# End pass of a graph layer and expert layer: the second choice's scaling goes to GpSimd, and the last addition of a batch comes one batch later

## The chip, the cores and the metric

One core of one Trainium2 chip runs the whole kernel. The time is the device time of one execution in microseconds (us); lower is better. All arithmetic is in fp32.

## The reference, cut to what matters

Two layers run over 6250 nodes with 256 features each. The first gathers sums, maxima and means of the edges of each node and puts them through a two-layer network. The second is a mixture of experts with 16 experts, of which each node uses two. Only the end of the second layer is touched by the change:

```python
# x is the first layer's output plus its input ("x1" in the kernel)
n = _layernorm(x)                                    # "x2" in the kernel
topk_vals, topk_idx = jax.lax.top_k(n @ gate_w + gate_b, 2)
topk_w = jax.nn.softmax(topk_vals, axis=-1)
moe = jnp.sum(topk_w[..., None] * sel, axis=2)       # sel: rows of the two chosen experts
y = n + moe
mu, var = jnp.mean(y, -1, keepdims=True), jnp.var(y, -1, keepdims=True)
out = x + (y - mu) / jnp.sqrt(var + 1e-5) * gamma + beta
```

## The kernel before, in words

The nodes are cut into 50 tiles of 125 nodes, two tiles to a pair of 250 nodes, 25 pairs. The kernel runs in four stages: scans over the edges, the first layer pair by pair, the experts over 113 slot tiles of 128 rows (their outputs are scattered to a DRAM tensor `expert_rows`, first choices in one half and second choices in the other), and the end pass, which is the last 110 us or so. Only the end pass is changed.

The end pass runs over 14 batches (`BATCHES`, L145), numbered 0 to 13. Batches 0, 9 and 13 have one pair (two tiles), the other eleven have two pairs (four tiles). The values x1 of all nodes lie already in SBUF (`FX1`). The order of the work on each engine is written out by hand, and counting semaphores tie the engines together. For a batch n:

- **SyncE** (`load_y`, L494 to L512) loads the two expert rows of each node into `FY[n % 4][0]` and `FY[n % 4][1]`. Both loads add to the same semaphore `fy_got`. Four batches are loaded ahead. In the loop it waits for `f_read` n + 1 and loads batch n + 4, then waits for `f_out` n + 1 and stores batch n, with two transfers.
- **ScalarE** (L950 to L979) writes the normed rows into PSUM (`normed_again`, `FS[n % 2]`, signals `f_x2`), takes the square root of the variances (`deviation`, `f_sd`), and norms the finished sum from `FS` into `FN[n % 2]` in SBUF (`last_norm`, `f_norm`). Its order is normed_again 0, normed_again 1, deviation 0, last_norm 0, normed_again 2, deviation 1, last_norm 1, normed_again 3, and so on.
- **VectorE** (L1552 to L1601) adds the weighted expert rows onto `FS` in place (`add_expert(n, 0)` and `add_expert(n, 1)`, one SCALAR_TENSOR_TENSOR of 256 columns for each tile, L1559), takes mean and variance (`moments`, L1568 and L1571, `f_var`), works out scale and shift (`scale_shift`, L1578 and L1580, `f_stat`), and adds `FN` and the residual rows `FZ` into `FO` (`finish`, L1589, `f_out`).
- **GpSimd** (`times_gamma`, L698 to L705) multiplies `FN[n % 2]` by gamma in place, after `f_norm`, and signals `f_scaled`. It does nothing else in the end pass.
- **TensorE** (`residual_rows`, L1194 to L1206) writes x1 + beta into PSUM, `FZ[n % 2]`: for each pair a product with the identity over 512 columns (L1199) and two products of one row of ones with beta over 256 columns (L1201). From batch 2 on it waits for `f_out` n - 1, that is for `finish(n - 2)`, as there are two buffers. It signals `f_z`, for which `finish(n)` waits.

The loop of VectorE is, for n from 0 to 13: `add_expert(n + 1, 0)`, `scale_shift(n)`, `add_expert(n + 1, 1)`, `moments(n + 1)`, `finish(n)`.

Of the kernel before, what the change touches and what calls it, by code (L numbers as in the profile page):

```python
# [21 lines left out]
ALU = mybir.AluOpType  # L22
# [80 lines left out]
def gnn_moe_kernel(nc, x, dst, edge_attr, u, gW1, gb1, gW2, gb2, gate_w, gate_b,  # L103
# [3 lines left out]
    GF = u.shape[1]  # L107
    HID = gW1.shape[1]
    NX, _, FF = ew1.shape
    NT = 125  # L110
    TILES = N // NT
# [33 lines left out]
    BATCHES = [(0, 1)] + [(n, n + 2) for n in range(1, EARLY_M - 1, 2)] + [(EARLY_M - 1, EARLY_M)] + [(n, min(n + 2, MACROS)) for n in range(EARLY_M, MACROS, 2)]  # L145
# [4 lines left out]
    DEEP = 4  # L150
# [24 lines left out]
    def block_at(n):  # L175
        return n + LATE_M if n < EARLY_M else n - EARLY_M
# [10 lines left out]
    with ExitStack() as ctx:  # L187
        def sem(name):
            return ctx.enter_context(nc.semaphore(name))
# [30 lines left out]
        wsel = k.take(2, TILES, parts=NT)  # L220
# [8 lines left out]
        slotf, second = (k.take(SLOT_TILES) for _ in range(2))  # L229
# [11 lines left out]
        a = Area(mem, KEPT, A1)  # L241
# [4 lines left out]
        a = Area(mem, A1, TOTAL)  # L246
# [32 lines left out]
        a = Area(mem, WORK + 12 * D, WORK_END)  # L279
# [12 lines left out]
        a = Area(mem, WORK_END, TOTAL)  # L292
        OL = [a.take(OB, P, parts=NT) for _ in range(HOT)]
        OH = [a.take(OB, KINDS, parts=NT) for _ in range(HOT)]
        a = Area(mem, WORK_END, TOTAL)
        w1now = [a.take(DC, FF) for _ in range(4)]

        a = Area(mem, KEPT, W2_AT)
# [15 lines left out]
        a = Area(mem, at, W2_AT)  # L314
# [8 lines left out]
        a = Area(mem, W_AT, WORK)  # L323
# [6 lines left out]
        a = Area(mem, WORK, WORK_END)  # L330
        FX1 = [a.take(2 * (m1 - m0), D) for m0, m1 in BATCHES]

        a = Area(mem, W2_AT, A1)
        FY = [[a.take(CB, D) for _ in range(2)] for _ in range(DEEP)]
# [9 lines left out]
        FS, FZ = ([ps[0:NT, (at + 2 * b) * 512:(at + 2 * b + 2) * 512].rearrange("p (a d) -> p a d", a=CB) for b in range(2)] for at in (0, 4))  # L344
# [39 lines left out]
        yo_stored = [sem(f"expert_rows_stored{i}") for i in range(2)]  # L384
        fx_got = sem("final_x1_got")
        fy_got = [sem(f"final_y_got{i}") for i in range(DEEP)]
        f_x2, f_step, f_read, f_var, f_sd, f_stat, f_norm, f_scaled, f_z, f_out = (sem(f"final_{n}") for n in ("x2", "step", "y_read", "var", "sd", "stat", "norm", "scaled", "residual", "out"))
        pads_zeroed = sem("pads_zeroed")
        out_stored = [sem(f"out_stored{i}") for i in range(2)]
        passed = sem("waits_passed")  # L390
# [10 lines left out]
        def spread(ap, axis, n):  # L401

            shape = list(ap.shape)
            shape.insert(axis, n)
            return ap.unsqueeze(axis).to_broadcast(shape)
# [112 lines left out]
        def _(pool):  # L518
# [176 lines left out]
            in_pairs(pool, SLOT_TILES, slots_step, ahead=5, first=SURE - 4)  # L695


            def times_gamma(n):  # L698
                a = 2 * (BATCHES[n][1] - BATCHES[n][0])
                pool.wait_ge(f_norm, n + 1)  # L700
                pool.tensor_tensor(FN[n % 2][:, 0:a], FN[n % 2][:, 0:a], spread(gammabc, 1, a), ALU.mult).then_inc(f_scaled, 1)
            pool.wait_ge(yo_stored[0], (SLOT_TILES - SLOT_TILES // 2) * 16)
            pool.wait_ge(yo_stored[1], SLOT_TILES // 2 * 16)
            for n in range(len(BATCHES)):
                times_gamma(n)  # L705


        @block.scalar
        def _(act):
# [240 lines left out]
            def normed_again(n):  # L950
                m0, m1 = BATCHES[n]
                if n >= 2:
                    act.wait_ge(f_norm, n - 1)
                for a in range(2 * (m1 - m0)):
                    j = 2 * block_at(m0) + a
                    ins = act.activation(FS[n % 2][:, a, :], FX1[n][0:NT, a, :], ACT.Identity, bias=nmr_2[:, j:j + 1], scale=rstd_2[:, j:j + 1])
                ins.then_inc(f_x2, 1)

            def deviation(n):
                tiles = 2 * (BATCHES[n][1] - BATCHES[n][0])  # L960
                act.wait_ge(f_var, n + 1)
                act.activation(sdc[n % 2][:, 0:tiles], mvc[n % 2][:, 0:tiles, 1], ACT.Sqrt, bias=epsc[0:NT]).then_inc(f_sd, 1)

            def last_norm(n):
                m0, m1 = BATCHES[n]
                act.wait_ge(f_stat, n + 1)
                if n >= 2:
                    act.wait_ge(f_out, n - 1)
                for a in range(2 * (m1 - m0)):
                    ins = act.activation(FN[n % 2][:, a, :], FS[n % 2][:, a, :], ACT.Identity, bias=nmc[n % 2][:, a:a + 1], scale=rsc[n % 2][:, a:a + 1])  # L970
                ins.then_inc(f_norm, 1)
            act.wait_ge(y_ready, SLOT_TILES + 2)
            act.wait_ge(fx_got, len(BATCHES) * 16)
            normed_again(0)
            for n in range(len(BATCHES)):
                if n + 1 < len(BATCHES):
                    normed_again(n + 1)
                deviation(n)
                last_norm(n)  # L979


        @block.tensor
# [227 lines left out]
        def _(dve):  # L1210
# [338 lines left out]
            in_pairs(dve, SLOT_TILES, expert_step, ahead=2, first=SURE)  # L1549


            def add_expert(n, kk):  # L1552
                m0, m1 = BATCHES[n]
                b = n % 2
                if kk == 0:
                    dve.wait_ge(f_x2, n + 1)
                    dve.wait_ge(fy_got[n % DEEP], (n // DEEP + 1) * 32)
                for a in range(2 * (m1 - m0)):
                    f1.mark(dve.scalar_tensor_tensor(out=FS[b][:, a, :], in0=FY[n % DEEP][kk][0:NT, a, :], scalar=wsel[:, kk, 2 * block_at(m0) + a:2 * block_at(m0) + a + 1],  # L1559
                                                     in1=FS[b][:, a, :], op0=ALU.mult, op1=ALU.add))  # L1560
                f1.wait()
                if kk == 1:
                    dve.sem_inc(f_read, 1)

            def moments(n):
                b, tiles = n % 2, 2 * (BATCHES[n][1] - BATCHES[n][0])
                for a in range(tiles):
                    f1.mark(dve.bn_stats(statc[b][:, a, :], FS[b][:, a, :]))  # L1568
                f1.wait()
                for a in range(tiles):  # L1570
                    f1.mark(dve.bn_aggr(mvc[b][:, a, :], statc[b][:, a, :]))  # L1571
                f1.wait()
                dve.sem_inc(f_var, 1)

            def scale_shift(n):
                b, tiles = n % 2, 2 * (BATCHES[n][1] - BATCHES[n][0])
                dve.wait_ge(f_sd, n + 1)
                f1.mark(dve.reciprocal(rsc[b][:, 0:tiles], sdc[b][:, 0:tiles]))  # L1578
                f1.wait()
                dve.scalar_tensor_tensor(out=nmc[b][:, 0:tiles], in0=mvc[b][:, 0:tiles, 0], scalar=-1.0, in1=rsc[b][:, 0:tiles],  # L1580
                                         op0=ALU.mult, op1=ALU.mult).then_inc(f_stat, 1)

            def finish(n):
                tiles = 2 * (BATCHES[n][1] - BATCHES[n][0])
                dve.wait_ge(f_scaled, n + 1)
                dve.wait_ge(f_z, n + 1)
                if n >= 2:
                    dve.wait_ge(out_stored[n % 2], n // 2 * 32)
                dve.tensor_tensor(FO[n % 2][:, 0:tiles], FN[n % 2][:, 0:tiles], FZ[n % 2][:, 0:tiles], ALU.add).then_inc(f_out, 1)  # L1589
            f1 = Steps(dve, f_step)  # L1590
            add_expert(0, 0)
            add_expert(0, 1)
            moments(0)
            for n in range(len(BATCHES)):
                if n + 1 < len(BATCHES):
                    add_expert(n + 1, 0)
                scale_shift(n)
                if n + 1 < len(BATCHES):
                    add_expert(n + 1, 1)
                    moments(n + 1)  # L1600
                finish(n)  # L1601


# [25 lines left out]
```

## Time and profile before

| | us |
|---|---|
| median of 3 runs | 1328.63 |
| lowest and highest | 1326.2 and 1332.45 |
| profiled execution, device time | 1334.45 |
| its span in the profile | 1332.7 |

The profiled execution is 5.8 us above the median, and 1.75 us of its device time lie around the span. In the page, busy time and instructions of each engine are:

```profile
PE 1185.9 (89%) x6684; PEld 1003.7 (75%) x6685; DVE 788.0 (59%) x3039; ACT 646.1 (48%) x1969; POOL 773.3 (58%) x1061
```

PE is TensorE, PEld its weight loads, DVE VectorE, ACT ScalarE, POOL GpSimd and SP SyncE. These shares are averages over all four stages; the end pass takes one twelfth of the span, so its own windows have to be read. L12 is line 12 of the kernel. The granted clock of TensorE is given as a share of 2.4 GHz.

### The profile page before, as it was taken

How to read it: one execution, taken by the hardware profiler on the slowest of the kernel's cores; microseconds unless marked ns; L12 is line 12 of the kernel's file. 1: busy time of each engine (PE TensorE's matmuls, PEld its weight loads, DVE VectorE, ACT ScalarE, POOL GpSimd, SP SyncE). 2: the span in 40 equal slices, each digit the busy share in tenths (PEclk: the TensorE clock that was granted, in tenths of full speed). 3: DMA queues.
4: the chain of work that ended last, by engine and by line, in shares of the span. 5: the costliest groups of instructions: out<-in, count | busy, mean ns of one | idle time of the engine just before them, and what ended most of it. 6: DMA issues, size and time to landing. Idle time of an engine off the chain costs nothing.

```text
span 1332.7 us, 28448 instructions
## 1 busy us (share of the span) xinstructions
PE 1185.9 (89%) x6684; PEld 1003.7 (75%) x6685; DVE 788.0 (59%) x3039; ACT 646.1 (48%) x1969; POOL 773.3 (58%) x1061
## 2 busy tenths in 40 slices
PE   2003999999999999999999989999999999999798
PEld 1003888888888888878888888899999999997343
DVE  4999999899799899903534014542222222222886
ACT  5963556655665665655664332223333333333554
POOL 4876666666666667666754235556666666663222
PEclk7555999999999999989999989999999999998555
DMA  9986677768758775592110348856666666664763
GB/s 313 287 269 232 201 275 284 283 237 318 256 215 294 276 239 189 218 334 80 47 45 28 115 155 296 269 174 205 212 212 204 211 212 211 210 212 123 244 203 93
DMA packets 131029, 282.67 MB, mean 212 GB/s; under 512 B 25609, under 2 KB 38283, under 8 KB 130821
## 3 DMA queue, kind: packets, MB, share of 16 engines
q1 hardware_dynamic: 93937, 218.40, 48.3%
q0 software_dynamic: 26048, 43.47, 10.4%
q10 hardware_dynamic: 10964, 19.96, 4.4%
q8 instruction: 23, 0.38, 0.1%
q14 instruction: 57, 0.47, 0.1%
HBM read 167.27 MB, written 114.25 MB: 211 GB/s over the span
## 4 chain that ended last, share of the span: by engine, by line
PE 63%; DMA 10%; issue 9%; POOL 8%; ACT 7%; POOLq 2%; DVE 1%; ACTq 1%; SPq 0%; DVEq 0%
PE ps L1158 14%; PE ps L1166 13%; PE ps L1048 8%; PE ps L1034 7%; PE ps L1036 7%; DMA mem<-piece_carry,mem 4%; PE ps L1199 3%; PE ps L1201 3%; POOL mem L571 2%; POOL mem L572 2%; PE ps L1144 2%; DMA mem<-x_normed,mem 2%; DMA mem<-in_dst_dram,mem 2%; POOL mem L554 2%; ACT mem L728 1%
## 5 line engine op out<-in xcount | busy, mean ns | idle before, releaser
L924 ACT ACTIVATE mem<-ps,mem 128x128 f32<-128x128 f32 x452 | 128.9, 368 | 306.8 <-PE ps L1158 304.8
L1158 PEld LDWEIGHTS ps<-mem 128*128 128x128 f32 x1808 | 221.4, 194 | 7.9 <-issue 3.0
L1158 PE MATMUL ps<-mem 128*128 128x128 f32 x1808 | 223.9, 278 | 1.5 <-issue 1.5
L1034 PE MATMUL ps<-mem 128*128 128x250 f32 x800 | 208.5, 383 | 13.5 <-ACT mem L826 11.9
L1166 PE MATMUL ps<-mem 128*128 x904 | 215.7, 382 | 2.8 <-issue 2.6
L1253 DVE TENSOR_TENSOR_SCAN mem<-ps,mem 128x80 f32<-128x80 f32 x960 | 207.9, 297 | 0.3
L1257 DVE TENSOR_TENSOR_SCAN mem<-ps,mem 128x80 f32<-128x80 f32 x960 | 207.8, 302 | 0.0
L1036 PE MATMUL ps<-mem 128*128 128x250 f32 x800 | 204.4, 378 | 0.0
L664 POOL DMA_INDIRECT expert_rows<-mem x113 | 113.5, 1004 | 126.9 <-DVE mem L1515 112.6
L1048 PE MATMUL ps<-mem 128*125 128x256 f32 x800 | 181.0, 379 | 0.7 <-ACT mem L826 0.7
L1166 PEld LDWEIGHTS ps<-mem 128*128 128x128 f32 x904 | 163.5, 191 | 22.7 <-issue 4.9
L1034 PEld LDWEIGHTS ps<-mem 128*128 128x128 f32 x800 | 152.7, 194 | 33.2 <-ACT mem L826 14.2
L1036 PEld LDWEIGHTS ps<-mem 128*128 128x128 f32 x800 | 153.8, 192 | 18.6
L1048 PEld LDWEIGHTS ps<-mem 128*125 128x125 f32 x800 | 146.3, 188 | 21.1 <-ACT mem L826 1.1
L1508 DVE COPY mem<-ps 128x256 f32<-128x256 f32 x113 | 47.8, 424 | 178.2 <-PE ps L1144 175.9
L1515 DVE TENSOR_TENSOR mem<-ps,mem 128x256 f32<-128x256 f32 x113 | 47.9, 424 | 171.1 <-PE ps L1166 160.3
L658 POOL DMA_INDIRECT mem<-x_normed,mem x113 | 112.7, 998 | 35.4 <-issue 13.0
L1015 PE MATMUL ps<-mem 125*128 125x125 f32 x100 | 20.6, 288 | 90.5 <-ACT mem L812 90.5
L826 ACT ACTIVATE mem<-ps,mem 128x250 f32<-128x250 f32 x200 | 77.0, 467 | 48.6 <-PE ps L1038 48.6
L571 POOL DMA_INDIRECT mem<-run_max,mem x50 | 63.6, 1272 | 46.5 <-issue 46.5
L1015 PEld LDWEIGHTS ps<-mem 125*128 125x128 f32 x100 | 11.6, 145 | 97.7 <-issue 97.7
L554 POOL DMA_INDIRECT mem<-in_dst_dram,mem x50 | 62.1, 1241 | 29.7 <-ACT mem L745 14.7
(252 smaller groups left out, 1696.1 us busy)
## 6 DMA issues: line engine op xcount, KB each, us to landing
mem<-in_L_ffn_w_dram SPq DMA_DIRECT2D x129, 512.0 KB, 9.4
run_sum<-mem SPq DMA_DIRECT2D x80, 480.0 KB
run_max<-mem SPq DMA_DIRECT2D x80, 480.0 KB
mem<-in_edge_attr_dram SPq DMA_DIRECT2D x72, 480.0 KB, 8.0
mem<-expert_rows SPq DMA_DIRECT2D x22, 512.0 KB, 5.4
x_rows<-mem ACTq DMA_DIRECT2D x25, 256.0 KB, 4.0
x_normed<-mem ACTq DMA_DIRECT2D x25, 256.0 KB
mem<-in_x_dram ACTq DMA_DIRECT2D x24, 256.0 KB, 4.1
```

Of the source, the lines that this page charges most:

```text
L554: pool.indirect_dma_start(out=SR[:, slot % RING, :], out_offset=None, in_=dst2, in_offset=bass.IndirectOffsetOnAxis(rowU[:, j:j + 1], 0)). ...
L571: pool.indirect_dma_start(out=GM[b][:, a, :], out_offset=None, in_=s_max[0:edges], in_offset=last).then_inc(gathered[b], 16)
L658: pool.indirect_dma_start(out=XG[b], out_offset=None, in_=x2_d[0:rows], in_offset=bass.IndirectOffsetOnAxis(slot_now[b], 0)).then_inc(xg_g ...
L664: pool.indirect_dma_start(out=ya_d, out_offset=bass.IndirectOffsetOnAxis(into_now[b], 0), in_=YO[b], in_offset=None).then_inc(yo_stored[b] ...
L924: ins = act.activation(hT[b][:, c, :], bank(2 + b, c * P, (c + 1) * P), ACT.Relu, bias=eb1c[:, bass.ds(e, 1), c])
L1034: pe.matmul(h, W1x[:, c, hc * P:(hc + 1) * P], XT[b][:, c, :], start=(c == 0), stop=False)
L1036: pe.matmul(h, W1a[:, s, hc * P:(hc + 1) * P], AT[b][:, s, :], start=False, stop=False)
L1048: ins = pe.matmul(bank(5, a * D, (a + 1) * D, NT), H[:, hc, a * NT:(a + 1) * NT], W2[:, hc, :], start=(hc == 0), stop=(hc == HC - 1))
L1158: ins = pe.matmul(bank(2 + b, f * P, (f + 1) * P), w1now[q][:, c, f * P:(f + 1) * P], XgT[b][:, c, :], start=(c == 0), stop=(c == DC - 1))
L1166: ins = pe.matmul(bank(6 + b, 0, D), hT[b][:, c, :], w(c * D, D), start=(c == 0), stop=(c == FC - 1))
L1253: ins = dve.tensor_tensor_scan(out=Sb[:, ::-1, f], data0=keep[b][:, ::-1], data1=Eb[b][:, ::-1, f], initial=0.0, op0=ALU.mult, op1=ALU.add)
L1257: ins = dve.tensor_tensor_scan(out=Eb[b][:, ::-1, f], data0=bound[b][:, ::-1], data1=Eb[b][:, ::-1, f], initial=-FMAX, op0=ALU.min, op1=AL ...
```

## The change

VectorE no longer multiplies the second choice's rows by their weights. GpSimd does this in place in `FY[n % 4][1]`, one `tensor_scalar` of 256 columns for each tile, two batches ahead of its multiplication by gamma. VectorE then adds these rows to the whole batch in one TENSOR_TENSOR of 1024 columns (512 in a short batch). Both additions of a batch now come together, before the scale and shift of the batch before it. `finish(n)` comes one round of the loop later, after the moments of batch n + 2. The lines of ScalarE are written in another way.

```diff
+            def weigh_second(n):
+                m0, m1 = BATCHES[n]
+                pool.wait_ge(fy_got[n % DEEP], (n // DEEP + 1) * 32)
+                for a in range(2 * (m1 - m0)):
+                    j = 2 * block_at(m0) + a
+                    ins = pool.tensor_scalar(FY[n % DEEP][1][0:NT, a, :], FY[n % DEEP][1][0:NT, a, :], wsel[:, 1, j:j + 1], None, ALU.mult)
+                ins.then_inc(f_second, 1)
...
+            weigh_second(0)
+            weigh_second(1)
             for n in range(len(BATCHES)):
+                if n + 2 < len(BATCHES):
+                    weigh_second(n + 2)
                 times_gamma(n)
...
             normed_again(0)
+            normed_again(1)
             for n in range(len(BATCHES)):
-                if n + 1 < len(BATCHES):
-                    normed_again(n + 1)
                 deviation(n)
                 last_norm(n)
+                if n + 2 < len(BATCHES):
+                    normed_again(n + 2)
...
-            def add_expert(n, kk):
+            def add_experts(n):
                 m0, m1 = BATCHES[n]
-                b = n % 2
-                if kk == 0:
-                    dve.wait_ge(f_x2, n + 1)
-                    dve.wait_ge(fy_got[n % DEEP], (n // DEEP + 1) * 32)
-                for a in range(2 * (m1 - m0)):
-                    f1.mark(dve.scalar_tensor_tensor(out=FS[b][:, a, :], in0=FY[n % DEEP][kk][0:NT, a, :], scalar=wsel[:, kk, 2 * block_at(m0) + a:2 * block_at(m0) + a + 1],
+                b, tiles = n % 2, 2 * (m1 - m0)
+                dve.wait_ge(f_x2, n + 1)
+                dve.wait_ge(fy_got[n % DEEP], (n // DEEP + 1) * 32)
+                for a in range(tiles):
+                    j = 2 * block_at(m0) + a
+                    f1.mark(dve.scalar_tensor_tensor(out=FS[b][:, a, :], in0=FY[n % DEEP][0][0:NT, a, :], scalar=wsel[:, 0, j:j + 1],
                                                      in1=FS[b][:, a, :], op0=ALU.mult, op1=ALU.add))
                 f1.wait()
-                if kk == 1:
-                    dve.sem_inc(f_read, 1)
+                dve.wait_ge(f_second, n + 1)
+                f1.mark(dve.tensor_tensor(FS[b][:, 0:tiles], FS[b][:, 0:tiles], FY[n % DEEP][1][0:NT, 0:tiles], ALU.add))
+                f1.wait()
+                dve.sem_inc(f_read, 1)
...
-            add_expert(0, 0)
-            add_expert(0, 1)
+            last = len(BATCHES) - 1
+            add_experts(0)
             moments(0)
             for n in range(len(BATCHES)):
-                if n + 1 < len(BATCHES):
-                    add_expert(n + 1, 0)
+                if n < last:
+                    add_experts(n + 1)
                 scale_shift(n)
-                if n + 1 < len(BATCHES):
-                    add_expert(n + 1, 1)
+                if n < last:
                     moments(n + 1)
-                finish(n)
+                if n:
+                    finish(n - 1)
+            finish(last)
```

## Rows read from the trace of the kernel before

**Rows 1.** Windows of 10 or 20 us, with the view's own head line.

```profile
core 0: us, PE busy (x) PEld busy (x) DVE busy (x) ACT busy (x) POOL busy (x), PEclk, DMA share, GB/s
1200.00:1220.00 20.00, 20.00 (x137) 18.73 (x136) 4.24 (x10) 5.70 (x20) 8.27 (x14) 1.00 0.35 101
...
1230.00:1240.00 10.00, 3.09 (x6) 1.14 (x4) 7.17 (x23) 3.35 (x7) 1.08 (x1) 0.50 1.01 361
...
1250.00:1260.00 10.00, 10.00 (x16) 3.96 (x15) 9.02 (x28) 6.42 (x14) 2.25 (x2) 0.50 0.70 213
```

**Rows 2.** Chain that ended last, from 1240 us: start us, us, what.

```profile
1240.48 0.70 DVE mem L1589
...
1241.23 2.07 PE ps L1199 x2
1243.30 2.00 PE ps L1201 x4
...
1327.16 2.01 PE ps L1201 x4
...
1329.26 0.69 DVE mem L1589
```

**Rows 3.** Timeline, batch 1: start, us, engine, line, out<-in, xcount, [idle before <-releaser].

```profile
1234.65 1.66 DVE L1559 SCALAR_TENSOR_TENSOR ps<-mem,ps 125x256 f32<-125x256 f32 x4 [2.36 <-DMA mem<-expert_rows]
...
1236.74 1.02 ACT L970 ACTIVATE mem<-ps,mem 125x256 f32<-125x256 f32 x2 [4.07 <-DVE mem L1580]
1237.80 2.04 ACT L956 ACTIVATE ps<-mem 125x256 f32<-125x256 f32 x4
...
1238.43 1.42 DVE L1568 BATCH_NORM_STATS2 mem<-ps 125x6 f32<-125x256 f32 x4 [0.15 <-DVE ps L1559]
```

**Rows 4.** Timeline, one settled round of the end pass.

```profile
1257.74 1.93 ACT L970 ACTIVATE mem<-ps,mem 125x256 f32<-125x256 f32 x4 [3.05 <-DVE mem L1580]
...
1259.71 2.04 ACT L956 ACTIVATE ps<-mem 125x256 f32<-125x256 f32 x4
...
1261.78 1.22 DVE L1589 TENSOR_TENSOR mem<-mem,ps 125x1024 f32<-125x1024 f32 x1 [0.51 <-POOL mem L701]
...
1262.92 1.66 DVE L1559 SCALAR_TENSOR_TENSOR ps<-mem,ps 125x256 f32<-125x256 f32 x4
...
1264.61 0.18 DVE L1578 RECIPROCAL mem<-mem 125x4 f32<-125x4 f32 x1
1264.82 0.16 DVE L1580 SCALAR_TENSOR_TENSOR mem<-mem 125x4 f32<-125x4 f32 x1
...
1265.02 1.93 ACT L970 ACTIVATE mem<-ps,mem 125x256 f32<-125x256 f32 x4 [3.05 <-DVE mem L1580]
```

**Rows 5.** Timeline, batch 12 at the end of the pass.

```profile
1322.86 2.00 POOL L701 TENSOR_TENSOR mem<-mem 125x1024 f32<-125x1024 f32 x1 [4.50 <-ACT mem L970]
...
1325.26 1.22 DVE L1589 TENSOR_TENSOR mem<-mem,ps 125x1024 f32<-125x1024 f32 x1 [2.46 <-PE ps L1201]
```

**Rows 6.** GpSimd groups by shape: out<-in, xcount | busy us, mean ns | idle before.

```profile
L582 POOL TENSOR_TENSOR mem<-mem 125x192 f32<-125x192 f32 x25 | 14.8, 592 | 15.7 <-ACT mem L782 15.7
...
L591 POOL TENSOR_SCALAR mem<-mem 125x2 f32<-125x2 f32 x25 | 4.9, 195 | 2.4 <-ACT mem L796 0.6
...
L544 POOL TENSOR_SCALAR mem<-mem 125x50 f32<-125x50 f32 x1 | 0.4, 373 | 0.0
...
L541 POOL TENSOR_SCALAR_AFFINE_SELECT mem<-mem 125x125 f32<-125x125 f32 x1 | 0.3, 289 | 0.0
...
L617 POOL TENSOR_TENSOR mem<-mem 125x512 f32<-125x512 f32 x25 | 32.7, 1310 | 3.5 <-POOL mem L600 2.4
...
L619 POOL TENSOR_TENSOR mem<-mem 125x512 f32<-125x512 f32 x25 | 27.3, 1091 | 2.0
```

**Rows 7.** DMA issues by line: KB each, median us from issue to landing.

```profile
mem<-expert_rows SPq DMA_DIRECT2D x22, 512.0 KB, 5.4
```

**Rows 8.** Timeline, TensorE's first product of the end pass.

```profile
1222.53 1.12 PE L1199 MATMUL ps<-mem 125*125 125x512 f32 x2 [2.01 <-DVE mem L1515]
```

More of the change, by code:

```diff
@@ L386, in gnn_moe_kernel @@
         fy_got = [sem(f"final_y_got{i}") for i in range(DEEP)]
-        f_x2, f_step, f_read, f_var, f_sd, f_stat, f_norm, f_scaled, f_z, f_out = (sem(f"final_{n}") for n in ("x2", "step", "y_read", "var", "sd", "stat", "norm", "scaled", "residual", "out"))
+        f_x2, f_second, f_step, f_read, f_var, f_sd, f_stat, f_norm, f_scaled, f_z, f_out = (sem(f"final_{n}") for n in ("x2", "second", "step", "y_read", "var", "sd", "stat", "norm", "scaled", "residual", "out"))
         pads_zeroed = sem("pads_zeroed")
```

## The prediction

> **What bounds the kernel now.** I read the windows first, since only the last 110 us change. While the experts run, TensorE is busy 20.00 of 20 us at clock 1.00. In the end pass its clock is 0.50, which is 1.2 GHz; it has a gap around 1230 to 1240, and from 1241 on it is busy 10.00 of 10 us again, still at 0.50. VectorE, at 9.02 of 10, looks nearly as full [rows 1]. The chain that ended last decides between the two. It leaves VectorE at 1241.2, behind the first `finish` (0.70 us from 1240.48), and then stays on TensorE, one piece of L1199 (2.00 us, the first 2.07) and one of L1201 (2.00 us) for each pair, to 1329.17. There are 22 such pairs (25 less the three of batches 0 and 1, done before): 1329.17 - 1241.23 = 87.94 us, 4.00 us each. Behind it come one `finish` and the last store [rows 2]. So the end pass ends when TensorE does, and TensorE is started by `finish(0)`, as `residual_rows(2)` needs the PSUM buffer which that reads. The VectorE loop has its own pace: from one `last_norm` to the next 1265.02 - 1257.74 = 7.28 us, against 7.99 us that TensorE takes for two pairs [rows 2, 4]. It is faster, so it is not the bound, and a cheaper VectorE round gains nothing. The reader is to ask of this diff only when `finish(0)` comes, and whether a round stays below 7.99 us.
>
> **The change, part by part.**
>
> *ScalarE.* Written out, the new order is the same sequence as the old. Cost 0; nothing moves.
>
> *Scaling on GpSimd.* No row has a `tensor_scalar` of 256 columns on GpSimd. From below: one of 2 columns takes 0.195 us, and the one-input AFFINE_SELECT of 125 columns 0.289, so 0.76 ns a column and 0.39 us for 256. From above: the TENSOR_SCALAR of 50 columns takes 0.373, so 3.7 ns a column and 1.13 us. The row nearest in size is the TENSOR_TENSOR of 192 columns at 0.592; with one input less but a third more columns I take 0.60 us, 2.4 us for a batch, and keep 0.39 and 1.13 [rows 6]. With gamma's 2.00 us [rows 5] this is 4.4 us a batch (6.5 at most) against a round of 7.5: in the settled rounds it is hidden by the slack of GpSimd, as a batch is weighed almost a round before VectorE adds it. It is not hidden in batch 1. Its rows land at 1234.65, when VectorE starts at once [rows 3], and GpSimd can start no sooner.
> The Trainium skill, "GPSIMD Engine Reference", section 4.1, says that one-input operations on GpSimd run at about line rate; by that the 256 columns would cost near the low end, and the sum below would be +6.3 instead of +7.1.
>
> *Start of the pass.* Batch 1's first addition runs 1234.65 to 1236.31 [rows 3]. The scaling runs to 1234.70 + 2.40 = 1237.10, so the large addition waits. No row has a TENSOR_TENSOR of 1024 columns written to PSUM; the one of `finish` reads SBUF and PSUM like it and takes 1.22 us [rows 4]. Ends: 1.2, and 1.66 if it ran at the pace of the four instructions that it replaces; I take 1.22. It ends at 1238.37. Behind a sum the next instruction starts after about 0.03 us (1264.58 to 1264.61), with a semaphore increment in between after 0.15 [rows 3, 4]. Scale and shift take 0.40 with the step to ScalarE, so `last_norm(0)` starts at 1238.9 where it started at 1236.74: +2.2. ScalarE then does `last_norm(0)` and `normed_again(2)`, which ended at 1239.84 and now ends at 1242.0 [rows 3].
>
> *finish(0) a round later.* `add_experts(2)` starts at 1242.05: 1.66, a step of 0.05, 1.22, a step of 0.15, scale and shift; `moments(2)` starts at 1245.45. From the start of `moments(1)` to the `finish` behind it took 1240.48 - 1238.43 = 2.05 us, so `finish(0)` starts at 1247.5 instead of 1240.48 [rows 2, 3], and TensorE at 1248.2 instead of 1241.23: **+7.0 us**. What it waited for besides is early (gamma and the residual rows of batch 0). That is nearly a whole round of delay put straight on the chain.
>
> *The settled round.* From one `last_norm` to the next: 1.93 + 2.04 on ScalarE with steps, until `normed_again` ends 4.01 later (1261.75 - 1257.74), 0.05, the four products 1.66, 0.05, the large addition 1.22, 0.15, scale and shift 0.41: 7.55 us [rows 4]. Before, `finish` filled the place in which the large addition now stands, so the round does not shrink, it grows by 0.27. Against 7.99 for TensorE it still fits, by 0.44. `finish(1)` ends at about 1256.3, where TensorE would be free for batch 3 at 1248.2 + 7.99 = 1256.2: +0.1. From there VectorE draws ahead.
>
> *Loads and stores.* Batch n + 5's load now stands behind the store of batch n, a round later. It lands 5.4 us after its issue [rows 7], about 7 us after that `finish` with the store's issues ahead of it. That is some 1 us before GpSimd gets to it and a round before VectorE does. Cost 0; if this cover went, GpSimd would start the scaling later and still have about 3 us before VectorE waits.
>
> *End.* With two finishes left (12 and 13), VectorE waits for TensorE, as before; the last wait, the last `finish` and the store are unchanged. The large additions save VectorE 0.44 us a batch, off the chain: 0.
>
> *Sum.* +7.0 + 0.1 = +7.1 us on the profiled execution, 1334.45 to about 1341.6 (span 1339.8). The change is local and the median lies 5.8 us below the profiled one for reasons outside the pass, so I put it on the median: 1328.63 + 7.1 = 1335.7. By the ends of the scaling's cost: at 0.39 the first addition of 1.66 us is what is waited for, 0.75 less, +6.3; at 1.13 it is 4 x 0.53 = 2.1 more, +9.2. If the large addition takes 1.66, another 0.9 (it counts in batches 1 and 2).
>
> **Rivals.**
>
> *B, TensorE gets its clock back and stops being the bound; not slower.* The first product of the pass took 1.12 us for its two halves at a clock still near 1 [rows 8], against 2.07 [rows 2], so a pair would take about 2.1 us. Then VectorE's loop sets the end: from `last_norm(1)` at 1245.5, eight rounds of 7.55, and with the short batches two of about 5.3 and one of 6.6, `last_norm(12)` starts at 1323.1; 1.97 of it, 2.00 of gamma and 1.2 of `finish(12)` later the last `finish` starts at 1328.3, against 1329.26 now [rows 2, 5]: -1.0 us, 1327.6. It decides once a pair takes less than (1328.3 - 1248.2) / 22 = 3.64 us. Against it: through 88 us without a gap the clock stayed at 0.50 [rows 1, 2], and the work is the same. The Trainium skill, "TensorE: Matmul & The Clock Gate", Part 1, says that sustained activity releases the throttle; by that rule this rival would come true, and this trace speaks against it.
>
> *C, VectorE's loop becomes the bound; slower still.* GpSimd's new reads and writes beside VectorE could stretch both. GpSimd's own sums of one shape differ by 20% with their surroundings (1.310 against 1.091 us) [rows 6]. 20% on the VectorE part of the round, 3.3 us, makes it 8.2: TensorE then waits in each round, and the end is some 2.5 to 3 us later, 1338.5; twice that stretch gives 1343. For it: the margin is only 0.44 us. Against: `finish` already runs beside nothing unusual, and the products keep 1.66 in all rounds shown, with GpSimd busy or not.
>
> *D, the later `finish` costs nothing* because something else starts TensorE; then the time stays at 1328 to 1329. I see nothing that could: the wait for `f_out` is the one in the code, and the chain shows it.
>
> **How the numbers follow.** A measurement of this kernel tells about 0.5% from no change, 6.6 us. The forecast case A (TensorE the bound, started a round later) has 0.82, B 0.06, C 0.09, D 0.03. A runs from +6.3 to +9.2 with its middle just above the border; the three runs of before spread over 6 us, which blurs it. In A I give 0.6 to over 0.5%. So slower 0.82 x 0.6 + 0.09 = 0.58, same 0.40, faster 0.02 (only B with luck). A alone spans 1334.9 to 1337.8; with the large addition's high end, the spread of a median and the milder half of C, the range is 1332.5 to 1340.0.
>
> **What would show it.** Right: the chain still runs on L1199 and L1201, in 22 pairs of 4.00 us, but from about 1248.2; L1589's first row starts near 1247.5; rounds of L970 are 7.5 us apart; the addition of batch 1 waits about 0.8 us for GpSimd. The scaling's mean duration reads off its term. Wrong: a clock above 0.50 after 1241, a chain with VectorE or GpSimd in the rounds, rounds above 8 us, or a first `finish` before 1246.

## The result, and the profile after the change

The changed kernel takes 1337.92 us (median of 4 runs, 1337.0 to 1339.7) against 1328.6 us: a ratio of 1.0069 with a 95% interval of 1.0042 to 1.0096. It is slower by 9.3 us. The profiled execution took 1337.0 us, its span is 1335.3 us. Runs more than 1.5% above the fastest of their kernel are left out of all ratios.

The moment at which the end pass begins differs by some us from one execution to the next, for reasons ahead of it: here it begins 5.5 us earlier than in the profiled execution of before. So I measure the pass by itself, from the first residual product of TensorE to the end of the span: 1332.7 - 1222.53 = **110.2 us** before and 1335.3 - 1217.03 = **118.3 us** after. The change costs 8.1 us in the pass. L1199 and L1201 are now L1212 and L1214, the addition of the first choice's rows is L1572, the large one L1576, scale and shift L1593 and L1595, `finish` L1604, the scaling L703, gamma L709, `last_norm` L982 and `normed_again` L968.

The chain of the changed kernel, in order of time (start us, us, what), shows where TensorE's long stretch begins and ends:

```profile
1222.06 6.76 DMA mem<-expert_rows
...
1228.90 3.63 POOL mem L703 x4
...
1232.62 1.25 DVE ps L1576
...
1234.41 1.03 ACT mem L982 x2
...
1235.46 2.05 ACT ps L968 x4
...
1243.71 2.07 PE ps L1212 x2
1245.78 2.00 PE ps L1214 x4
...
1329.71 2.01 PE ps L1214 x4
```

From 1243.71 to 1331.72 it is TensorE alone, 22 pairs in 88.01 us, as it was 87.94 us before [rows 2]. Behind it come 3.6 us, as before. Ahead of it everything has moved: from the start of the pass to `residual_rows(2)` it is 1243.71 - 1217.03 = 26.68 us, where it was 1241.23 - 1222.53 = 18.70 [rows 2, 8]. The difference, 7.98 us, is the result but for 0.1. New in this part of the chain are four instructions of GpSimd, the large additions of batches 1 and 2 (the first of them waits for GpSimd), and batch 2's normed rows, additions and moments, which now stand ahead of `finish(0)`.

The timeline of the changed kernel shows the two halves of this stretch (start us, us, engine, line, operation, [idle before]):

```profile
1228.92 1.66 DVE L1572 SCALAR_TENSOR_TENSOR ps<-mem,ps 125x256 f32<-125x256 f32 x4 [0.78 <-DMA mem<-expert_rows]
1232.62 1.23 DVE L1576 TENSOR_TENSOR ps<-ps,mem 125x1024 f32<-125x1024 f32 x1 [2.04 <-POOL mem L703]
...
1234.41 1.02 ACT L982 ACTIVATE mem<-ps,mem 125x256 f32<-125x256 f32 x2 [5.88 <-DVE mem L1595]
...
1242.97 0.69 DVE L1604 TENSOR_TENSOR mem<-mem,ps 125x512 f32<-125x512 f32 x1 [0.23 <-DVE mem L1586]
...
1243.71 2.07 PE L1212 MATMUL ps<-mem 125*125 125x512 f32 x2 [16.51 <-DVE mem L1604]
...
1248.55 1.93 ACT L982 ACTIVATE mem<-ps,mem 125x256 f32<-125x256 f32 x4 [3.30 <-DVE mem L1595]
...
1251.76 0.49 PEld L1212 LDWEIGHTS ps<-mem 125*125 125x125 f32 x2 [0.72 <-DVE mem L1604]
1251.77 2.07 PE L1212 MATMUL ps<-mem 125*125 125x512 f32 x2
...
1256.08 1.93 ACT L982 ACTIVATE mem<-ps,mem 125x256 f32<-125x256 f32 x4 [3.30 <-DVE mem L1595]
```

First half: from the first addition of batch 1 to `last_norm(0)` it is 5.49 us (1228.92 to 1234.41), where it was 2.09 [rows 3]: +3.40. VectorE stood idle for 2.04 us before the large addition, until GpSimd was done. Second half: from `last_norm(0)` to TensorE it is 9.30 us, where it was 4.49: +4.81, the later `finish(0)`. The rows landed 0.2 us sooner after the start of the pass; 3.40 + 4.81 - 0.23 = 7.98. A round is 1256.08 - 1248.55 = 7.53 us, against 7.28 [rows 4].

The windows of the changed kernel say the same in another way:

```profile
1234.00:1243.00 9.00, 0.00 (x0) 0.00 (x0) 7.03 (x26) 5.22 (x12) 6.76 (x8) 0.50 0.17 64
1243.00:1331.00 88.00, 87.29 (x131) 35.94 (x132) 66.65 (x168) 44.49 (x96) 56.49 (x49) 0.50 0.52 163
```

The same stretch of the kernel before:

```profile
1242.00:1329.00 87.00, 87.00 (x132) 35.46 (x130) 72.28 (x212) 46.71 (x100) 24.12 (x13) 0.50 0.53 167
```

The columns are those of [rows 1]. TensorE, the bound of the pass, does nothing from 1234 to 1243. Later it is full, at 0.50 still. VectorE is down from 72.28 us of work to 66.65: the change did take work from VectorE, and that bought nothing.

### The profile page after: what moved, and what is told of

Same layout as the page of the kernel before. It is cut to its first block, busy times and chain, and to the rows that moved or that the text cites. A ratio compares the mean times of both kernels' runs of the same rounds, so it can differ in the third digit from the quotient of the medians.

```text
span 1335.3 us, 28463 instructions
## 1 busy us (share of the span) xinstructions
PE 1183.8 (89%) x6684; PEld 1000.8 (75%) x6685; DVE 784.7 (59%) x3003; ACT 646.5 (48%) x1969; POOL 820.0 (61%) x1111
## 4 chain that ended last, share of the span: by engine, by line
PE 64%; DMA 9%; issue 9%; POOL 8%; ACT 7%; POOLq 2%; DVE 1%; ACTq 1%; SPq 0%; DVEq 0%
PE ps L1171 14%; PE ps L1179 14%; PE ps L1061 8%; PE ps L1047 7%; PE ps L1049 7%; DMA mem<-piece_carry,mem 4%; PE ps L1212 3%; PE ps L1214 3%; DMA mem<-in_dst_dram,mem 2%; POOL mem L572 2%; POOL mem L571 2%; PE ps L1157 2%; ACT mem L740 1%; POOL mem L554 1%; PE ps L1097 1%
## 5 line engine op out<-in xcount | busy, mean ns | idle before, releaser
L1171 PE MATMUL ps<-mem 128*128 128x128 f32 x1808 | 221.1, 276 | 1.3 <-issue 1.2
```

The lines of the kernel that those rows point to most:

```text
L1171: ins = pe.matmul(bank(2 + b, f * P, (f + 1) * P), w1now[q][:, c, f * P:(f + 1) * P], XgT[b][:, c, :], start=(c == 0), stop=(c == DC - 1))
```

## The experiments

Twelve more kernels ran. The ratio is that to the kernel before, from runs on the same chip. The pass is measured in one profiled execution of each. Three pairs of kernels have the same pass (e5 and e12, e6 and e11, e7 and e9), and their passes differ by 0.5 to 0.8 us, so a difference below 1 us tells nothing by itself.

| kernel | pass, us | ratio (95%) |
|---|---|---|
| before | 110.2 | 1 |
| the change | 118.3 | 1.0069 (1.0042 to 1.0096) |
| e1 the change, finish in its own round | 126.3 | 1.0149 (1.0119 to 1.0178) |
| e2 before, finish a round later | 115.5 | 1.0057 (1.0034 to 1.0080) |
| e3 the change, finish(0) alone early | 119.1 | 1.0063 (1.0035 to 1.0092) |
| e4 the change, scaling as one product | 117.1 | 1.0040 (1.0012 to 1.0068) |
| e5 the change, one product a pair, x1 over 125 partitions | 111.1 | 1.0185 (1.0145 to 1.0226) |
| e6 before, the same | 108.9 | 1.0203 (1.0158 to 1.0247) |
| e7 split additions, the same | 101.1 | 1.0129 (1.0092 to 1.0166) |
| e8 split additions | 116.0 | 1.0120 (1.0059 to 1.0182) |
| e9 split additions, one product a pair | 101.7 | 0.9941 (0.9920 to 0.9962) |
| e10 before, finish later, one product a pair | 103.2 | 0.9947 (0.9927 to 0.9966) |
| e11 before, one product a pair | 108.3 | 1.0000 (0.9982 to 1.0019) |
| e12 the change, one product a pair | 111.9 | 1.0009 (0.9980 to 1.0039) |

### e1 and e2: the later finish, with and without the rest

e1 is the changed kernel with this:

```diff
-                if n:
-                    finish(n - 1)
-            finish(last)
+                finish(n)
```

> The pass is measured from TensorE's first residual product to the end of the span: 110.2 us before, 118.3 us after the change. This kernel keeps GpSimd's scaling and the large addition, and puts finish(n) back into its own round. Theory (TensorE at 4.00 us a pair is the bound, and a round must stay below 7.99 us): a finish in its own round waits for gamma and stands ahead of both additions, so a round is about 4.0 + 1.1 + 1.7 + 1.3 + 0.6 = 8.7 us; VectorE's loop becomes the bound, and the pass is about 126 us. Rival (the later finish alone costs the time, the rest is hidden): TensorE starts a round earlier and the pass is 112 us.

Measured: pass 126.3 us. The timeline of e1 shows the round:

```profile
1243.85 1.93 ACT L982 ACTIVATE mem<-ps,mem 125x256 f32<-125x256 f32 x4 [3.57 <-DVE mem L1595]
...
1245.86 2.00 POOL L709 TENSOR_TENSOR mem<-mem 125x1024 f32<-125x1024 f32 x1 [2.54 <-ACT mem L982]
...
1247.89 1.22 DVE L1604 TENSOR_TENSOR mem<-mem,ps 125x1024 f32<-125x1024 f32 x1 [2.33 <-POOL mem L709]
...
1249.17 1.22 PE L1212 MATMUL ps<-mem 125*125 125x512 f32 x1 [0.61 <-DVE mem L1604]
```

VectorE waits 2.33 us for gamma, and TensorE then waits for VectorE; in its chain one `last_norm` follows the other at 1252.51, 1261.39, 1270.06 and 1278.72, 8.7 to 8.9 us apart. With both additions ahead of scale and shift, the later finish is needed to keep the round below TensorE's 7.99 us.

e2 is the kernel before with `finish(n - 1)` in place of `finish(n)`, for n above 0, and the last one behind the loop.

> The kernel before with one edit: finish(n) comes one round later; both additions stay on VectorE as eight products. Theory: TensorE starts about 5.8 us later than in the kernel before, the round shrinks from 7.28 to about 7.0 us with no gain from it, the pass is about 116 us against 110.2. Rival (VectorE's loop sets the end): 13 rounds shorter by 0.3 us each, the pass is 106 to 108 us.

Measured: 115.5 us. The later finish alone costs 5.3 us, though it shortens VectorE's round (from one `last_norm` to the next 7.0 us in place of 7.28). The rows of batch 1 landed 0.5 us sooner after the start of the pass than in the kernel before (11.58 against 12.12 us); from there on the cost is 5.9 us, by a theory of 5.8.

### e3: is it the first finish?

```diff
-                if n:
-                    finish(n - 1)
+                if n != 1:
+                    finish(n - 1 if n else 0)
```

> The changed kernel, with finish(0) alone put back into round 0; all others stay a round later. If the start by finish(0) is what costs, as the prediction put it, TensorE starts 6 us earlier and the pass is about 112.5 us. If every finish releases a TensorE batch and rounds of 7.5 us are hardly shorter than TensorE's 7.99, then batch 3 waits for finish(1) at the same time as now, and the pass stays at 118.3, plus 0.3 for the finish put ahead of the next addition: 118.6 us.

Measured: 119.1 us. The timeline of e3:

```profile
1237.63 1.02 ACT L982 ACTIVATE mem<-ps,mem 125x256 f32<-125x256 f32 x2 [6.56 <-DVE mem L1595]
...
1240.43 0.69 DVE L1604 TENSOR_TENSOR mem<-mem,ps 125x512 f32<-125x512 f32 x1 [1.09 <-POOL mem L709]
...
1241.17 2.07 PE L1212 MATMUL ps<-mem 125*125 125x512 f32 x2 [10.76 <-DVE mem L1604]
...
1255.25 2.07 PE L1212 MATMUL ps<-mem 125*125 125x512 f32 x2 [6.01 <-DVE mem L1604]
```

TensorE started 3.5 us after `last_norm(0)` in place of 9.3, worked through batch 2, and then stood for 6.01 us until `finish(1)`. Nothing was gained; the 0.8 us more than the changed kernel are in part the rows of batch 1, which landed 0.5 us later here. So it is not `finish(0)` alone: every finish releases one batch of TensorE, and as rounds of 7.5 us are hardly shorter than TensorE's 7.99, a start gained at `finish(0)` is lost again at `finish(1)`. What costs is that the whole series is a round late.

### e4: a cheaper scaling

```diff
-                for a in range(2 * (m1 - m0)):
-                    j = 2 * block_at(m0) + a
-                    ins = pool.tensor_scalar(FY[n % DEEP][1][0:NT, a, :], FY[n % DEEP][1][0:NT, a, :], wsel[:, 1, j:j + 1], None, ALU.mult)
-                ins.then_inc(f_second, 1)
+                a = 2 * (m1 - m0)
+                j = 2 * block_at(m0)
+                pool.tensor_tensor(FY[n % DEEP][1][0:NT, 0:a, :], FY[n % DEEP][1][0:NT, 0:a, :], spread(wsel[:, 1, j:j + a], 2, D), ALU.mult).then_inc(f_second, 1)
```

> The changed kernel, with GpSimd's four tensor_scalar of 256 columns (0.905 us apart) replaced by one tensor_tensor of 1024 columns with the weights spread over them. If it takes gamma's 2.00 us, the large addition of batch 1 starts 1.6 us earlier, and so does all behind it: pass 116.6 us. If GpSimd's scaling in batch 1 is not on the chain: 118.3, no change.

Measured: 117.1 us. The timeline of e4, batch 1:

```profile
1226.34 1.89 POOL L703 TENSOR_TENSOR mem<-mem 125x1024 f32<-125x1024 f32 x1 [3.19 <-DMA mem<-expert_rows]
1226.37 1.66 DVE L1571 SCALAR_TENSOR_TENSOR ps<-mem,ps 125x256 f32<-125x256 f32 x4 [1.22 <-DMA mem<-expert_rows]
...
1228.33 1.23 DVE L1575 TENSOR_TENSOR ps<-ps,mem 125x1024 f32<-125x1024 f32 x1 [0.30 <-POOL mem L703]
1229.02 1.89 POOL L703 TENSOR_TENSOR mem<-mem 125x1024 f32<-125x1024 f32 x1 [0.79 <-DMA mem<-expert_rows]
...
1229.92 1.01 DVE L1594 SCALAR_TENSOR_TENSOR mem<-mem 125x2 f32<-125x2 f32 x1
...
1230.96 1.02 ACT L981 ACTIVATE mem<-ps,mem 125x256 f32<-125x256 f32 x2 [5.43 <-DVE mem L1594]
```

The scaling of a batch takes 1.89 us in place of 3.62, and VectorE's wait falls from 2.04 to 0.30 us. That is on the chain, as expected. But from the first addition to `last_norm(0)` it is 4.59 us (1226.37 to 1230.96) in place of 5.49: only 0.9 of the 1.7 us are left, since L1594 took 1.01 us where it takes 0.16 in most rounds; it ended when GpSimd's next product did (more on this below). The other 0.3 of the 1.2 us in the pass come from the rows, which landed that much sooner.

### e5 to e8: TensorE's work taken away, and the additions split

In e5 to e7 a pair has one product: beta lies as a 126th row under x1, and the identity has a row of ones below it.

```diff
-                    pe.matmul(pair, ident[0:NT, 0:NT], FX1[n][0:NT, 2 * m:2 * m + 2].rearrange("p a d -> p (a d)"), start=True, stop=False)
-                    for a in range(2):
-                        ins = pe.matmul(pair[:, a * D:(a + 1) * D], ones[0:1, 0:NT], betabc[0:1], start=False, stop=(a == 1))
+                    ins = pe.matmul(pair, plus_row[0:NT + 1, 0:NT], FX1[n][0:NT + 1, 2 * m:2 * m + 2].rearrange("p a d -> p (a d)"), start=True, stop=True)
...
-                sp.dma_start(FX1[n].rearrange("p (i a) d -> p i a d", a=2), batch_rows(x1_d, m0, m1)).then_inc(fx_got, 16)
+                sp.dma_start(FX1[n][0:NT].rearrange("p (i a) d -> p i a d", a=2), batch_rows(x1_d, m0, m1)[0:NT]).then_inc(fx_got, 16)
+                sp.dma_start(FX1[n][NT:NT + 1], spread(row(beta, 1), 1, 2 * (m1 - m0))).then_inc(fx_got, 16)
```

> The changed kernel with half of TensorE's work in the pass taken away and the result kept: beta is laid as a 126th row under x1 in SBUF, so one product with an identity that has a row of ones below it gives x1 + beta, and the two products of one row (2.00 us a pair) go. Theory (TensorE is the bound after the change, at 4.00 us a pair): a pair takes 2.0 us, VectorE's loop of 7.53 us sets the end, and the pass falls from 118.3 to about 110.1 us. Rival (VectorE's loop is already the bound, TensorE only runs beside it): the pass stays at 118.3 us.

> The same edit on the kernel before. Theory: there VectorE's loop of 7.28 us ends only some 0.7 us ahead of TensorE, so the pass falls from 110.2 to 109.5 us only. With e5 it gives what the change costs where TensorE is no bound: about +0.6 us instead of +8.1. Rival (the change costs its 8 us on VectorE): e5 minus e6 stays at 8 us.

In e7 and e8 the large addition has a function of its own, `add_second`, which stands behind `scale_shift(n)`:

```diff
                 if n < last:
-                    add_experts(n + 1)
+                    add_first(n + 1)
                 scale_shift(n)
                 if n < last:
+                    add_second(n + 1)
                     moments(n + 1)
```

> The changed kernel with one product a pair, and with the large addition behind scale_shift(n), where the second addition stood before. Theory: nothing is left on the way from the normed rows to scale and shift but the first addition, VectorE is busy all the time, a round is 6.5 us, and the pass is 99 us, against 110.2 in the kernel before: about 11 us (0.8%) faster than it. If GpSimd's work beside VectorE or the later loads bind first, a round is 7 us or more and the pass 104 us or more.

> The same order of the additions as in e7, but with TensorE's full work of 4.00 us a pair. Theory: rounds of 6.5 us are of no use, only the time of the first finish counts, which is 1.5 us earlier than in the changed kernel: pass 116.8 us. If VectorE's loop counted: 107 us or less.

In the pass, all four came out near the theory: 111.1, 108.9, 101.1 and 116.0 us, for 110.1, 109.5, 99 and 116.8. Halving TensorE's work took 7.2 us from the changed kernel and 1.3 from the kernel before, so e5 is 2.2 us behind e6, where the change is 8.1 behind. That is more than the 0.6 us expected: the change is not free where TensorE is no bound, its rounds are 7.5 us there against 7.3. e8 shows the other side: shorter rounds with TensorE's full work give 116.0 us.

With TensorE's full work the runs now form a row: 110.2 us before, 115.5 with the later finish alone (e2), 116.0 with GpSimd's scaling and the large addition besides (e8), 118.3 when the large addition also stands ahead of scale and shift (the change). The later finish is the largest step, the order of the two additions costs 2.3 us, and moving the scaling to GpSimd costs 0.5 us by itself, which is less than a pass can tell; it is that order which puts GpSimd's time ahead of `last_norm(0)`.

But in whole e5 to e7 were slower, by 1.3 to 2.0%, which no theory had expected. The windows of e5 and of the kernel before from 800 to 900 us, while the experts run and x1 is loaded:

```profile
800.00:900.00 100.00, 76.05 (x493) 67.07 (x492) 40.42 (x124) 19.57 (x69) 43.27 (x71) 0.98 0.66 206
```

```profile
800.00:900.00 100.00, 95.25 (x658) 87.31 (x658) 48.21 (x151) 25.89 (x92) 55.11 (x92) 1.00 0.73 247
```

TensorE loses 19 us there, and among the waits of e5 in this stretch is one of TensorE for expert weights, which the kernel before has not (us in total, times, longest):

```profile
PEld ps L1177 <- DMA mem<-in_L_ffn_w_dram: 21.2, 8, 3.4
```

The expert weights share SyncE's queue with the loads of x1, and these were cut to 125 partitions and joined by 14 small ones. The timeline of SyncE's queue in e5 shows where the queue stood, at a load (L476) and the small transfer behind it (L477):

```profile
808.89 0.41 SPq L476 DMA_DIRECT2D mem<-x_rows  x1
809.35 5.50 SPq L477 DMA_DIRECT2D mem<-in_L_ffn_beta_dram  x1
```

Issuing the small ones took 0.7 to 5.5 us, 4.2 us in the median, and the weights behind them had to wait. e8 has none of this. Its pass is as expected, while its four runs reach from 1335.7 to 1356.3 us (the profiled one 1338.2), so its ratio says little of the pass; where its longer runs lost time was not seen, and stays open.

### e9 to e12: the same with the loads as they were

The loads of x1 span 128 partitions again, and one transfer after them writes beta into the unused row:

```diff
+            sp.wait_ge(fx_got, len(BATCHES) * 16)
+            sp.dma_start(mem[NT:NT + 1, WORK:WORK + TILES * D].rearrange("p (t d) -> p t d", d=D), spread(row(beta, 1), 1, TILES)).then_inc(fx_got, 16)
```

> As e7, but the loads of x1 span 128 partitions again, as in the kernel before, and the row of beta is written over the unused 126th row by one transfer after them. Theory: what made e5 to e7 long lies ahead of the pass, in the loads of x1 over 125 partitions, which held up the weights' queue between 800 and 900 us; with them undone the pass starts at 1215 to 1223 us again and lasts 101 us as in e7: 1318 to 1321 us, 0.6 to 0.8% faster than the kernel before. Rival (the loads are not the cause): it stays above 1340 us.

> The kernel before with two edits: finish(n) a round later (as e2) and one product a pair in this way. Both additions stay on VectorE, GpSimd scales nothing. Theory: VectorE is the bound at 6.96 us of work a round, pass about 105 us, 1323 us in all. If the later finish is a loss whatever TensorE costs: 115 us as in e2.

> The kernel before with one product a pair in this way: pass 109 us as in e6, and the time within 0.2% of the kernel before, as VectorE's loop of 7.28 us ends only 1 us ahead of TensorE there.

> The changed kernel with one product a pair in this way: pass 110 to 111 us as in e5, and some 7 us faster than the changed kernel in whole, 1330 us. If TensorE is not what bounds the changed kernel: 1338 us.

Measured: medians of 1321.7, 1325.75, 1328.56 and 1331.98 us, passes of 101.7, 103.2, 108.3 and 111.9 us. The time lost ahead of the pass is gone. In the trace of e5 it went with the issue of the small transfers; whether it was theirs or came of the loads over 125 partitions just ahead of them wasn't told apart. e12 came out 1 us above its 110 to 111, and is 3.6 us behind e11 in the pass and 3.4 in whole: with TensorE's work halved, some of the change's cost remains, but less than half. e9 and e10 beat the kernel before, by 0.59% and 0.53%, and with it the change. The chain of e9 shows what bounds it in its long rounds:

```profile
1248.64 1.94 ACT mem L989 x4
1250.60 2.04 ACT ps L975 x4
1255.31 1.95 ACT mem L989 x4
1257.28 2.04 ACT ps L975 x4
1262.02 1.94 ACT mem L989 x4
```

These are rounds of 6.7 us, ScalarE's two parts with VectorE's first addition and scale and shift between them; no TensorE. With TensorE out of the way the later finish is a gain (e10 against e11: 5.1 us of the pass), where it was a loss of 5.3 us with it (e2 against before).

## Why the prediction was right, and where it was off

*The bound.* Right: TensorE at 4.00 us a pair carried most of the result, and the work saved on VectorE bought nothing. e5 and e12 show it by taking half of TensorE's work away: of 8.1 us, 2.2 (e5 against e6) and 3.6 (e12 against e11) are left.

*The later finish.* The +4.8 us from `last_norm(0)` to TensorE were predicted as 1238.9 to 1248.2, 9.3 us, and measured at 9.30. But the step "TensorE is started by `finish(0)`" was too narrow. e3 shows that `finish(1)` and those behind it count as much; the prediction had the near tie at batch 3 in its sum as +0.1 (0.07 measured), and did not draw the conclusion.

*The scaling's cost.* This term was too small. I took 0.60 us for 256 columns from the nearest row; the spacing of four is 3.62 / 4 = 0.905 us, inside the ends of 0.39 and 1.13 [rows 6]. That is 1.2 us more in batch 1, and all of it is on the chain: VectorE waited 2.04 us, not 0.8. With it the sum is +8.3 us; the rows of batch 1 landed 0.2 us sooner, and that gives the 8.1 measured in the pass. The 50-column row of the same operation was the better guide than a row of like size of another operation. The rule of the Trainium skill ("GPSIMD Engine Reference", section 4.1: one-input operations at about line rate) would have made the sum +6.3, by 0.39 us an instruction; this trace disagrees with its 0.905, and the measurement decides.

*The round.* 7.55 us predicted, 7.53 measured; the large addition took 1.23 us for my 1.22. ScalarE's change was none.

*The loads.* "Cost 0" held for the changed kernel, but barely. In e12, where TensorE no longer hides it, a load and the scaling behind it are in the chain after the short batch:

```profile
1290.89 5.50 DMA mem<-expert_rows
1296.49 3.62 POOL mem L710 x4
```

*The rivals.* B did not come: the clock stayed at 0.50. Its price, worked out as 1.0 us less than before, was too kind: e5 and e12 have the pass without TensorE's bound, and are 0.9 and 1.7 us longer than the pass before. C did not come, the round kept its margin. D did not come.

*The numbers.* 1335.7 us against 1337.92. One us of the difference is the scaling; the rest is within the spread of the runs. Slower by over 0.5% had 0.58, and came at 0.69%, but the interval of 0.42 to 0.96% holds the border too. On which side of it the ratio fell was in part luck, as the prediction said itself; the start of TensorE a round later was not.

## What to carry to other kernels

Look for the engine that the chain of waits runs on over the whole stage, and ask of each edit only when it moves that engine's start and its waits; a loop that is made cheaper beside it gains nothing, and a step put a round later costs most of a round if the buffers it frees feed the bound (5.3 us in e2, of a round of 7). The same edit can change its sign when the bound goes: here the later finish was worth -5 us or +5 us. When an operation moves to another engine, its steady share may be hidden while its first instance, at the start of a pipeline, is paid in full.

## What the runs showed of the hardware

- On GpSimd a TENSOR_SCALAR of 256 columns with a weight for each partition is slower for each column than a TENSOR_TENSOR: four took 3.62 us in the changed kernel, one TENSOR_TENSOR of the same 1024 columns with the weights spread 1.89 us (e4).
- VectorE's small scale-and-shift instruction, which has two inputs in SBUF, waits for a GpSimd TENSOR_TENSOR that is running. In the timeline of the changed kernel, at the last batch, both end together at 1323.1:

```profile
1321.07 2.00 POOL L709 TENSOR_TENSOR mem<-mem 125x1024 f32<-125x1024 f32 x1 [3.26 <-ACT mem L982]
1321.56 1.53 DVE L1595 SCALAR_TENSOR_TENSOR mem<-mem 125x2 f32<-125x2 f32 x1
```

  Beside GpSimd's TENSOR_SCALARs it depends on the moment. Here it started 0.18 us after one of them, took 0.31 us and ended 0.48 us after that start, long before the 0.905 us were over:

```profile
1290.19 3.62 POOL L703 TENSOR_SCALAR mem<-mem 125x256 f32<-125x256 f32 x4
...
1291.27 0.31 DVE L1595 SCALAR_TENSOR_TENSOR mem<-mem 125x4 f32<-125x4 f32 x1
```

  At 1255.88, 0.64 us after the start of one of four that began at 1252.55, it took its 0.16 us. In e8 it started 0.03, 0.07, 0.13 and 0.15 us after one and took 0.46, 0.42, 0.36 and 0.33 us, so it ended 0.49 us after that start each time. For TENSOR_TENSOR the wait lasted to the end in every case seen, in the changed kernel, e3, e4, e5, e7, e9, e10 and e12.

  The Trainium skill ("SBUF — State Buffer", "Who interferes with whom") says that a VectorE instruction with two SBUF inputs contends with a GpSimd instruction that reads SBUF. These traces agree, and show besides that with a TENSOR_SCALAR the wait ends 0.48 to 0.49 us after its start.
- TensorE's clock stayed at 0.50 (1.2 GHz) through 88 us without a gap, in which half of the time went to products with one row of ones (L1214). In e11, with products of 126 rows alone and TensorE busy half of the time, the mean clock of a window rose to 0.72 and 0.79; these are windows of e11:

```profile
1240.00:1250.00 10.00, 5.86 (x7) 2.19 (x8) 9.17 (x27) 4.31 (x10) 2.00 (x1) 0.50 0.61 192
1250.00:1260.00 10.00, 5.09 (x6) 1.07 (x5) 9.09 (x27) 6.88 (x15) 2.83 (x2) 0.72 0.71 225
1260.00:1270.00 10.00, 3.89 (x5) 1.41 (x6) 8.68 (x26) 5.58 (x13) 3.16 (x2) 0.79 0.49 156
```

  The rule that sustained activity brings the clock back (the Trainium skill, "TensorE: Matmul & The Clock Gate", Part 1) did not hold in the changed kernel, whose work has the products with one row in it. What sets it apart was not tested.
